# Three of eight dense expert blocks moved into the routing's search and product, the other five spread over ten sparse blocks

## The reference

```
x = layernorm(x + attention(x))            # 16 heads of 8, keys and values by way of a latent of 32
S = sigmoid(xt @ Wg).T                     # 8 experts, xt: 4096 x 128
G, I = top_k(S, k)                         # k = 1024: each expert takes its best 1024 tokens
hid = gelu(xt[I] @ W1 + b1)                # 512 hidden channels
out = (hid @ W2 + b2) * G
new_x = zeros.at[I].add(out)
x = layernorm(x + new_x)
```

## Time and profile before

| | |
|---|---|
| median of three runs | 630.24 us |
| the profiled execution: time, span | 630.24 us, 628.5 us |
| mean granted TensorE clock | 0.871 |
| busy over the span | TensorE 480.7, VectorE 336.3, ScalarE 281.9, GpSimd 276.4 us |
| first gather of the experts | 388.68 us |
| first expert matmul | 404.49 us |
| end of the last scatter's landing | 600.1 us |

### The profile page before, as it was taken

The page is one execution under the profiler, slowest core; times in us unless marked ns, Lnnn a source line. Parts: engine busy times, 40 slices in busy tenths (PEclk is TensorE's granted clock), DMA queues, the critical chain, the costliest instruction groups (busy, mean ns, idle before and its releaser), DMA issues.

```text
span 628.5 us, 9892 instructions
## 1 busy us (share of the span) xinstructions
PE 480.7 (76%) x3666; PEld 349.3 (56%) x3666; DVE 336.3 (54%) x874; ACT 281.9 (45%) x532; POOL 276.4 (44%) x327
## 2 busy tenths in 40 slices
PE   5327999999899999999983024899999999998000
PEld 3125667777677777777752013466666666776000
DVE  3627477767668687878825879412222222223055
ACT  2102566666566666656666403443333333333015
POOL 5364452727244352711000005774847474777700
PEclk9657899999899999999996555599999999999555
DMA  3555453543616352541040630222323333343364
GB/s 90 122 155 109 129 123 101 120 135 76 179 35 131 125 126 98 119 119 36 3 137 1 180 95 9 54 66 43 58 38 58 45 50 50 65 54 32 30 142 133
DMA packets 55837, 54.57 MB, mean 87 GB/s; under 512 B 14475, under 2 KB 47214, under 8 KB 54894
## 3 DMA queue, kind: packets, MB, share of 16 engines
q0 software_dynamic: 27280, 37.02, 27.6%
q1 hardware_dynamic: 25146, 15.26, 8.8%
q10 hardware_dynamic: 3364, 1.66, 0.9%
HBM read 29.86 MB, written 23.72 MB: 85 GB/s over the span
## 4 chain that ended last, share of the span: by engine, by line
PE 63%; DMA 13%; DVE 12%; ACT 5%; POOL 3%; issue 3%; POOLq 0%; ACTq 0%; DVEq 0%; SPq 0%
PE banks L769 9%; PE banks L755 9%; PE banks L902 8%; DMA q_stack<-shift_t 8%; PE banks L917 7%; PE banks L741 7%; PE banks L949 5%; PE banks L942 5%; DMA q_split<-q_lo 3%; DVE hT L1124 2%; POOL summed L528 2%; PE banks L700 2%; PE banks L705 2%; DVE hT L1194 1%; PE banks L697 1%
## 5 line engine op out<-in xcount | busy, mean ns | idle before, releaser
L609 ACT ACTIVATE probs<-banks 128x512 f32<-128x512 f32 x256 | 146.7, 601 | 118.5 <-PE banks L755 114.6
L999 DVE TENSOR_REDUCE row_max<-banks 128x2 f32<-128x512 f32 x256 | 167.1, 686 | 30.9 <-PE banks L741 28.9
L741 PE MATMUL banks<-k_stack,q_stack 128*128 128x256 f32 x512 | 121.9, 324 | 19.6 <-DMA q_stack<-q_split 19.6
L755 PE MATMUL banks<-q_stack,k_stack 128*128 128x256 f32 x512 | 109.4, 296 | 10.6 <-DMA q_stack<-shift_t 9.2
L528 POOL DMA_INDIRECT summed<-v_ones,index x56 | 87.9, 1569 | 42.7 <-DVE v_ones L1269 24.2
L741 PEld LDWEIGHTS banks<-k_stack,q_stack 128*128 128x128 f32 x512 | 82.4, 200 | 27.6 <-issue 25.3
L755 PEld LDWEIGHTS banks<-q_stack,k_stack 128*128 128x128 f32 x512 | 79.3, 192 | 20.7 <-DMA q_stack<-shift_t 11.0
L444 POOL DMA_DIRECT2D q_stack<-q_split x64 | 35.0, 553 | 91.6 <-PE banks L755 83.4
L769 PE MATMUL banks<-probs,v_ones 128*32 128x256 f32 x1024 | 70.0, 392 | 0.5 <-ACT probs L609 0.5
L518 POOL DMA_INDIRECT taken<-x_table,index x56 | 54.9, 981 | 28.0 <-issue 14.9
L639 ACT ACTIVATE hT<-banks,b_cols 128x512 f32<-128x512 f32 x56 | 37.5, 686 | 54.0 <-PE banks L902 54.0
(11 more groups left out here) (215 smaller groups left out, 624.7 us busy)
## 6 DMA issues: line engine op xcount, KB each, us to landing
q_stack<-q_split POOLq DMA_DIRECT2D x64, 128.0 KB, 3.0
k_stack<-k_split POOLq DMA_DIRECT2D x7, 1024.0 KB, 6.9
k_split<-k_hi POOLq DMA_DIRECT2D x16, 256.0 KB, 5.8
q_split<-q_hi POOLq DMA_DIRECT2D x16, 256.0 KB, 7.4
w_buf<-in_L_ffn_W SPq DMA_DIRECT2D x14, 256.0 KB, 2.8
x_table<-rows SPq DMA_DIRECT2D x1, 2176.0 KB, 14.6
k_split<-k_lo POOLq DMA_DIRECT2D x8, 256.0 KB, 11.2
q_split<-q_lo POOLq DMA_DIRECT2D x8, 256.0 KB, 10.8
```

The lines of the kernel that those rows point to most:

```text
L609: s.activation(probs[:, NR * (m % 2) + r], ps_second[:, head % 2], ACT.Exp, scale=SCALE).then_inc(exp_done, 1)
L741: mm = t_.matmul(ps_first[:, u % 3, i * SEQ:(i + 1) * SEQ], q_stack[:, b % SLOTS, r, gg, i * P:(i + 1) * P], k_stack[:, ring, gg, side], s ...
L755: mm = t_.matmul(ps_second[:, u % 2, j * SEQ:(j + 1) * SEQ], k_stack[:, ring, gg, side, j * P:(j + 1) * P], q_stack[:, b % SLOTS, r, gg], ...
L999: v.tensor_reduce(row_max[:, m % NG, 2 * r:2 * r + 2], ps_first[:, u % 3].rearrange("p (i j) -> p i j", i=2), AX, ALU.max).then_inc(first_ ...
```

## The change

Dense blocks 0 to 2 are called window blocks. TensorE computes them in pieces: 16 matmul pieces a block (8 of the first layer with 256 columns each, 8 of the second with two chunk matmuls each) and one transposition between blocks, 50 pieces in all. Three pieces stand behind each of the twelve search matmuls, eight behind the second prefix sum, six behind the first part of the first product. They use PSUM banks 0, 1, 2 and 4 and SBUF tiles whose attention contents are no longer needed. ScalarE copies the transposed block in, applies the gelus and copies the result out to `xc_all`; it scales the rows in groups between them, and makes the gate sigmoid ahead of the rows. VectorE adds bias and gate to the window blocks in the expert loop (`gate_window`). The other five dense blocks run one per two iterations: first layer in the odd one, second layer in the even one, a quarter behind each chunk of `down`.

```diff
-        SPARSE_BLOCKS, DENSE_BLOCKS = 2 * SPARSE, TILES // 4
+        SPARSE_BLOCKS, DENSE_BLOCKS = 2 * SPARSE, TILES // 4 - WINDOW
...
-            act.wait_ge(means_made, 1)
-            for t in range(TILES):
-                s.activation(rows[:, t, 0:D], xc_all[:, t], ACT.Identity, scale=rstd[:, t:t + 1],
-                             bias=neg_mean[:, t:t + 1]).then_inc(rows_scaled, 1)
             act.wait_ge(lg_made, 1)
             s.activation(rows[:, :, D:GATED], lg[:], ACT.Sigmoid).then_inc(gates_made, 1)
...
+            scale_rows(0, 4)
+            act.wait_ge(k_stored, 16 * TERMS * PAIRS)
+            act.wait_ge(q_stored, 16 * TERMS * PAIRS)
+            act.wait_ge(b1_out, 1)
+            for i in range(WINDOW):
+                act.wait_ge(window_turned, i + 1)
+                s.copy(window_x, window_turn).then_inc(window_copied, 1)
+                scale_rows(4 + 14 * i, 2)
+                for f in range(FBLK):
+                    act.wait_ge(window_up_full, FBLK * i + f + 1)
+                    col = FBLK * DENSE + f
+                    s.activation(window_h[f], window_up[f], ACT.Gelu, bias=b1_cols[:, col:col + 1]).then_inc(window_gelu, 1)
+                    scale_rows(6 + 14 * i + 3 * f, 3)
+                act.wait_ge(window_down_full, i + 1)
+                s.copy(xc_all[:, 4 * i:4 * i + 4].rearrange("p c d -> p (c d)"), window_down).then_inc(window_kept, 1)
...
-                if blk <= DENSE_BLOCKS:
-                    dense(blk - 1)
+                if blk % 2 and blk < 2 * DENSE_BLOCKS:
+                    dense(blk // 2)
...
+            def window_first(i, f, side):
+
+                if f == 0 and side == 0:
+                    if i == 0:
+                        pe.wait_ge(dense_w_in, 32)
+                    pe.wait_ge(window_copied, i + 1)
+                if side == 0:
+                    if f == 1 and i:
+                        pe.wait_ge(window_kept, i)
+                    elif f == 3 or i:
+                        pe.wait_ge(window_gelu, FBLK * i + 1 if f == 3 else FBLK * i)
+                cols = slice(side * SEQ, (side + 1) * SEQ)
+                mm = t_.matmul(window_up[f][:, cols], dense_w1[:, f * P:(f + 1) * P], window_x[:, cols], start=True, stop=True)
+                if side:
+                    mm.then_inc(window_up_full, 1)
+
+            def window_second(i, c, side):
+
+                if c == 0 and side == 0:
+                    pe.wait_ge(window_gelu, FBLK * i + FBLK)
+                for f in (2 * side, 2 * side + 1):
+                    mm = t_.matmul(window_down[:, c * P:(c + 1) * P], window_h[f][:, c * P:(c + 1) * P], dense_w2[:, f],
+                                   start=(f == 0), stop=(f == FBLK - 1))
+                if c == 3 and side:
+                    mm.then_inc(window_down_full, 1)
...
+            window_turn_rows(0)
             for n in range(SEARCH_STEPS):
                 pe.wait_ge(counted, 3 * n + 3)
                 t_.matmul(ps_pv[:, 0, 0:3], same_eb[:], counts[:], start=True, stop=True).then_inc(totalled, 1)
+                window_units(SEARCH_UNITS)
...
             prefix(sel, 1)
+            window_units(PRODUCT_UNITS[0])
...
+                        if (group, part) == (0, 1):
+                            window_units(PRODUCT_UNITS[1])
...
-                    if c and blk < DENSE_BLOCKS:
-                        dense_first(blk, c - 1)
+                    if c and blk % 2 == 0 and blk < 2 * DENSE_BLOCKS:
+                        dense_first(blk // 2, c - 1)
+                    if blk % 2 and blk < 2 * DENSE_BLOCKS:
+                        dense_second(blk // 2, c)
...
-                if 2 <= blk < DENSE_BLOCKS + 2:
-                    dense_first(blk - 2, FBLK - 1)
-                    dense_second(blk - 2)
+                if blk % 2 == 0 and blk <= 2 * DENSE_BLOCKS:
+                    dense_first(blk // 2 - 1, FBLK - 1)
...
-                if blk <= DENSE_BLOCKS:
-                    dense_turn(blk - 1)
+                if blk % 2 and blk < 2 * DENSE_BLOCKS:
+                    dense_turn(blk // 2)
                 down(blk - 1)
...
+                if blk % 2 and blk < 2 * DENSE_BLOCKS + 2:
+                    take_dense(blk // 2 - 1)
+                elif 2 <= blk // 2 < WINDOW + 2:
+                    gate_window(blk // 2 - 2)
```

More of the change, by code:

```diff
@@ L36 @@
 DENSE = SPARSE
+WINDOW = 3
+SEARCH_UNITS, PRODUCT_UNITS = 3, (8, 6)
 GROUPS = [(0, 2), (2, SPARSE - 2)]
@@ L241, in post_ln_layer @@
         dense_h, dense_x = probs[:, 0:FBLK], probs[:, FBLK]
+        window_h = (k_lo[:].bitcast(F32), q_lo[:].bitcast(F32), oT_raw[:].rearrange("p s i -> p (s i)"), kq_full[:, 0])
+        window_x = kq_full[:, 1]
+        window_turn, window_up, window_down = banks[:, 4], (banks[:, 0], banks[:, 1], banks[:, 2], banks[:, 0]), banks[:, 1]
+        window_turned, window_copied, window_up_full = sem("window_turned"), sem("window_copied"), sem("window_up_full")
+        window_gelu, window_down_full, window_kept = sem("window_gelu"), sem("window_down_full"), sem("window_kept")
+        window_biased = sem("window_biased")
         dense_bank = ps_pv.rearrange("p r i -> p (r i)")
@@ L271, in post_ln_layer @@
         SCATTERED = 16 * CHUNKS
-        SPARSE_BLOCKS, DENSE_BLOCKS = 2 * SPARSE, TILES // 4
+        SPARSE_BLOCKS, DENSE_BLOCKS = 2 * SPARSE, TILES // 4 - WINDOW
+        assert 2 * DENSE_BLOCKS <= SPARSE_BLOCKS
         block = ctx.enter_context(nc.Block())
@@ L612, in _, with scale_rows @@
             s.activation(rstd[:], var_all[:], ACT.Sqrt, bias=eps_col[:, 0:1], scale=1.0 / D).then_inc(var_rooted, 1)
-            act.wait_ge(means_made, 1)
-            for t in range(TILES):
-                s.activation(rows[:, t, 0:D], xc_all[:, t], ACT.Identity, scale=rstd[:, t:t + 1],
-                             bias=neg_mean[:, t:t + 1]).then_inc(rows_scaled, 1)
             act.wait_ge(lg_made, 1)
             s.activation(rows[:, :, D:GATED], lg[:], ACT.Sigmoid).then_inc(gates_made, 1)
+            act.wait_ge(means_made, 1)
+            def scale_rows(first, n):
+                for t in range(first, min(first + n, TILES)):
+                    s.activation(rows[:, t, 0:D], xc_all[:, t], ACT.Identity, scale=rstd[:, t:t + 1],
+                                 bias=neg_mean[:, t:t + 1]).then_inc(rows_scaled, 1)
+            scale_rows(0, 4)
[13 more added lines that the diff above has]
+                s.copy(xc_all[:, 4 * i:4 * i + 4].rearrange("p c d -> p (c d)"), window_down).then_inc(window_kept, 1)
+            assert 4 + 14 * WINDOW >= TILES
             for part in range(HOT_PARTS[1]):
@@ L627, in _ @@
                 ins.then_inc(hot_id_made[1], 1)
-            act.wait_ge(b1_out, 1)
             def gelu(blk, fs):
@@ L825, in _, with window_turn_rows @@
             t_.matmul(ps_a[:, 0:1], ones[0:1, :], bound[:], start=True, stop=True).then_inc(tensor_step, 1)
+            def window_turn_rows(i):
+                pe.wait_ge(rows_scaled, 4 * i + 4)
+                if i:
+                    pe.wait_ge(window_copied, i)
+                for c in range(4):
+                    mm = t_.transpose(window_turn[:, c * P:(c + 1) * P], rows[:, 4 * i + c, 0:D], ident[:])
+                mm.then_inc(window_turned, 1)
+            def window_first(i, f, side):
[12 more added lines that the diff above has]
+                    mm.then_inc(window_up_full, 1)
@@ new lines, in window_second @@
+            def window_second(i, c, side):
[6 more added lines that the diff above has]
+                    mm.then_inc(window_down_full, 1)
+            FIRST_UNITS, UNITS = 2 * FBLK, 4 * FBLK + 1
@@ new lines, in window_unit @@
+            def window_unit(u):
+                if u >= UNITS * WINDOW - 1:
+                    return
+                i, k = divmod(u, UNITS)
+                if k < FIRST_UNITS:
+                    window_first(i, k // 2, k % 2)
+                elif k == FIRST_UNITS and i + 1 < WINDOW:
+                    window_turn_rows(i + 1)
+                else:
+                    k -= FIRST_UNITS + (i + 1 < WINDOW)
+                    window_second(i, k // 2, k % 2)
+            unit = Count()
@@ L826, in _, with window_units @@
+            def window_units(n):
+                for _ in range(n):
+                    window_unit(unit.next() - 1)
+            window_turn_rows(0)
             for n in range(SEARCH_STEPS):
@@ L870, in _ @@
                             turn(0)
+                        if (group, part) == (0, 1):
+                            window_units(PRODUCT_UNITS[1])
+                            assert unit.value >= UNITS * WINDOW - 1
                         pe.wait_ge(hot_a_made, HOT_PARTS[0] * group + part + 1)
@@ L930, in dense_turn @@
                 for c in range(4):
-                    mm = t_.transpose(dense_bank[:, c * P:(c + 1) * P], rows[:, 4 * i + c, 0:D], ident[:])
+                    mm = t_.transpose(dense_bank[:, c * P:(c + 1) * P], rows[:, 4 * (WINDOW + i) + c, 0:D], ident[:])
```

(29 more changed lines are left out.)

## The result

The changed kernel takes 609.0 us in the median of four runs (607.64 to 611.95), a ratio of 0.966 to the kernel before (95% interval 0.961 to 0.972). The forecast was 612. The profiled execution is the slowest of the four, 611.95 us with a span of 610.2.

What follows compares the result with a forecast made beforehand. TensorE was taken to bound the kernel up to the fourth expert, GpSimd after that. 630.2 - 25.3 (expert stage) + 6.6 (search) + 0.4 (product) = 612 us; the range was 605 to 621, with chance 0.83 or so.

Steps and rivals of the forecast that it cites:

- What bounds the kernel: Whole path: TensorE up to the fourth expert, GpSimd after; TensorE's gain counts only as far as GpSimd can follow.
- The expert stage: Three dense blocks leave, five are spread out; GpSimd becomes the bound from 431 us and ends 25.3 us earlier.
- The first with 1 us to spare: Expert stage: block 3's outputs come at about 455.7 us, ahead of GpSimd's half scatter at 456.6.
- The search: Three pieces behind each search matmul: low clock for two steps, gelu waits and window changes add 6.6 us.
- the first wait for the fourth gelu: Search, window 0: TensorE waits for ScalarE's fourth gelu, with one table load of 1.28 us; +1.3 us.
- the change of window: Search, first to second window: down matmul, copy out, copy in and handovers exceed the slack; +0.9 us.
- the last: Search, second change of window, in the last step, ahead of the bounds' matmul with little slack; +1.4 us.
- The product: Fourteen pieces in TensorE's idle time ahead of the first two product parts; +0.4 us, bounds 0 and 4.1.
- the low clock: Rival, search and product: the pieces never lift the clock, or it falls at each wait; +16.4, 621 us; chance 0.16.
- Loads not hidden: Rival, search and product: each TensorE pass also pays its weight load, so pieces overrun; 619 us; chance 0.03.
- Table thrash: Rival, search: Identity row scalings between gelus swap ScalarE's table each time; two windows +22, 634 us; chance 0.04.
- Better overlap: Rival: the clock stays up into the first expert passes and ScalarE is ahead; 606 us; chance 0.08.

Runs made afterwards that it cites:

- e2: The changed kernel with the five dense blocks left out of the expert stage, with their copies and gelus; ratio to the kernel before 0.953.
- e3: The changed kernel with only the spreading undone: the five dense blocks start in iterations 1 to 5; ratio to the kernel before 0.990.
- e4: The changed kernel itself, unedited, run again on the other chips as a base; ratio to the kernel before 0.9645.
- e6: The changed kernel with four row scalings ahead of the gelus of windows 0 and 1 and ten behind them; ratio to the kernel before 0.962.
- e7: The changed kernel with two window blocks instead of three, none in the product, and six dense blocks among the experts; ratio to the kernel before 0.974.
- e10: The changed kernel with dense blocks starting one pair later and gelus ahead of the rows, together; ratio to the kernel before 0.957.
- e9: The changed kernel with GpSimd's gather of expert 1 moved behind the second index; ratio to the kernel before 0.964.
- e5: The changed kernel with the five dense blocks started one pair of sparse blocks later; ratio to the kernel before 0.960.

## Why the prediction was right, step by step

**What bounds the kernel:** right. TensorE up to the fourth expert, GpSimd behind it; e2 and e3 show it from both sides.

**The expert stage:** -25.3 predicted, -25.5 measured, and for the reason given. The pair lasts 22.97 (23.0), the gather of expert 3 comes 26.6 us behind the first expert matmul instead of 30.7 (4.1 earlier, 3.8 predicted), from there to the gather of expert 6 it is 521.30 - 438.02 = 83.3 (83.1). "The first with 1 us to spare" was right too: the outputs of block 3 were ready at 461.92 and their scatter started at 463.53, 1.6 later. It holds for this chip only. On the others, where TensorE starts 8 us later behind the first gather, the same kernel waits 8.28 us ahead of its first scatter, 3.96 ahead of gather 3 and twice for outputs (e4).

**The search:** +6.6 predicted, +3.3 in the steps and +1.4 ahead of the bounds, 4.7 measured; from the first to the last total it is 25.7 us, not 27 to 28. The mis-sized terms: one step at the lower clock, not two (0.76 for 1.5), and the first wait for the fourth gelu (0.63 for 1.3), because ScalarE loaded gelu's table while it would have waited anyway: the load ended 0.56 us before the first gelu's input came. The second such wait (1.14 for 1.5), the change of window (0.85 for 0.9) and the last (1.42 for 1.4) were near. That the rows make the gelu waits is shown by e6.

**The product:** +0.4 predicted, nothing measured: the fourteen pieces fit. The clock was down for the first of them, as assumed, and the gelu wait was 0.78 us (0.8). The first product ran at the upper clock, 0.66 us a part instead of 1.03, but that gained nothing: from its first part to the first gather it is 7.6 us before and after. What the routing did gain, 0.3 us, is the bounds' matmul, 0.29 us at the upper clock instead of 0.61.

**Sum:** the routing cost 4.4 instead of 7.0 us. The first chip's median of 609.0 is 3 below the forecast; the profiled execution of 611.95 agrees with it only because its attention took 2.5 us longer.

**The rivals:** the low clock did not decide. But it does come for a few microseconds: in five of the nine profiled executions with a window on the other chips (e2, e3, e4, e7, e10) it fell within the search, and such a trace lost about 1 to 2 us by it. Loads not hidden: a second-layer piece, four passes with four loads, starts every 0.45 us in the trace (from 355.46 to 356.35 four half pieces start, 0.22 apart), and first-layer pieces fitted three in 1.54. The Trainium skill, "TensorE: Matmul & The Clock Gate" (The mechanism, "What overlaps and what doesn't"), lets weight loads overlap running matmuls only where the row group differs; this trace does not agree. Table thrash: none. The Trainium skill, "ScalarE: Activation LUTs" (Table sets), puts identity in every set, and the trace agrees: no load stands between the row scalings and the gelus. Better overlap: no; the quicker product parts gained nothing, and the clock was down again by the first expert matmul.

## What to carry to other kernels

When the engine on the path hands its work to a second, nearly full one, read the second one's waits: their sum is the most that the first can give, and only where they stand. In e3 and e4, spreading the remaining work evenly added more than twice what moving three eighths of it away had brought before it. Work put into another engine's gaps costs what its own in-order waits add there, so let the engine that feeds it do that first and the filler last.

## What was not expected

- On the chips of the experiments VectorE and ScalarE stand still for 3.5 to 14 us during long bursts of indirect gathers, in the kernel before as in the changed one; on the first chip neither trace has it. Breaking up one burst shortened VectorE's stall and lengthened ScalarE's (e9).
- The granted clock can be lost in the search around waits of 1.16 (e2, e3, e10), 1.47 (e4) and 1.90 us (e7), though the first chip's trace held it through waits of 1.16 and 1.46. The length of the wait alone does not decide it.
- A table load of 1.28 us started before the input of its activation was there, ended 0.56 us before it, and cost nothing.
- The later start of the dense blocks (e5) removed 8 us of waits early in the stage and brought back most of them at its end.
